# The C product of chunk 15 moved from DVE to GpSimd in a selective-scan ring on one Trainium2 core

## What is computed

```python
xp = jnp.einsum('bld,rd->blr', x, x_proj_w)
dt_in = xp[..., :DT_RANK]
B = xp[..., DT_RANK:DT_RANK + D_STATE]
C = xp[..., DT_RANK + D_STATE:]
dt = jax.nn.softplus(jnp.einsum('blr,dr->bld', dt_in, dt_proj_w) + dt_proj_b)
dA = jnp.exp(dt[..., None] * A)
dBx = dt[..., None] * B[:, :, None, :] * x[..., None]
# step: h = dA_t * h + dBx_t;  y = einsum('bdn,bn->bd', h, C_t)
y = jnp.moveaxis(ys, 0, 1) + D * x
```

## Time and profile before

| | us |
|---|---|
| median of 3 runs | 7002.88 |
| lowest, highest | 6997.77, 7003.49 |
| profiled execution, its own time | 6997.07 |
| its span, first to last instruction | 6995.4 |

### The profile page before, as it was taken

How to read it: one execution, slowest core, us unless ns; L and a number is a source line. 1 busy time by engine, 2 the same in 40 slices (tenths; PEclk the granted TensorE clock), 3 DMA queues, 4 the chain that set the end, 5 groups by cost and what they waited for, 6 DMA issues and landing times. The chain is left out here.

```text
span 6995.4 us, 109105 instructions
## 1 busy us (share of the span) xinstructions
PE 5921.1 (85%) x32339; PEld 5392.8 (77%) x32339; DVE 6184.9 (88%) x6216; ACT 4956.5 (71%) x13239; POOL 5960.5 (85%) x3596
## 2 busy tenths in 40 slices
PE   4658688888888888888888888888888888888887
PEld 3424588888888888888888888888888888888887
DVE  7863799999999999999999999999999999999996
ACT  4536677777777777777777777777777777777774
POOL 3420899999999999999999999999999999999995
PEclk8779899999999999999999999999999999999999
DMA  2430212222122211222212221122211222112220
GB/s 61 97 71 5 78 59 74 74 78 74 54 74 74 79 70 58 74 74 78 72 56 74 74 79 69 59 74 74 78 69 59 74 74 78 66 57 75 77 73 30
DMA packets 96273, 479.74 MB, mean 69 GB/s; under 512 B 13089, under 2 KB 17329, under 8 KB 87410
## 3 DMA queue, kind: packets, MB, share of 16 engines
q1 hardware_dynamic: 95602, 471.63, 19.5%
HBM read 328.35 MB, written 143.24 MB: 67 GB/s over the span
## 5 line engine op out<-in xcount | busy, mean ns | idle before, releaser
L1026 POOL TENSOR_TENSOR s_ring<-s_bc,s_u_t 128x820 f32<-128x820 f32 x2048 | 3623.6, 1788 | 3.5 <-DMA s_bc<-rows_bc 3.5
L944 ACT ACTIVATE s_decay<-s_dt_t,a_neg 128x205 f32<-128x205 f32 x8192 | 3045.8, 420 | 751.9 <-DVE s_ring L1088 570.1
L846 PE MATMUL s_y_ps<-s_ring,ident 128*128 128x205 f32 x16384 | 3284.6, 350 | 168.5 <-POOL s_ring L1032 79.3
L846 PEld LDWEIGHTS s_y_ps<-s_ring,ident 128*128 128x128 f32 x16384 | 2946.3, 198 | 302.4 <-POOL s_ring L1032 103.4
L1032 POOL TENSOR_TENSOR s_ring<-s_ring,s_bc 128x820 f32<-128x820 f32 x1024 | 1974.4, 1928 | 403.3 <-DVE s_ring L1082 397.3
L1082 DVE TENSOR_TENSOR_SCAN s_ring<-s_decay,s_ring 128x820 f32<-128x820 f32 x1024 | 1900.6, 1856 | 186.1 <-ACT s_decay L944 184.3
L1082 DVE TENSOR_TENSOR_SCAN s_decay<-s_decay,s_ring 128x820 f32<-128x820 f32 x1024 | 1908.5, 1864 | 120.1 <-ACT s_decay L944 98.4
L877 PE MATMUL s_xch<-s_x_t,w_low 128*128 128x205 f32 x8192 | 1512.0, 337 | 1.7 <-ACT s_x_t L975 0.6
L877 PEld LDWEIGHTS s_xch<-s_x_t,w_low 128*128 128x128 f32 x8192 | 1432.9, 190 | 5.8 <-DVE s_h L1144 1.1
L1088 DVE TENSOR_TENSOR s_ring<-s_decay,s_bc 128x820 f32<-128x820 f32 x1024 | 1035.6, 1011 | 35.2
L988 ACT ACTIVATE s_y_t<-s_xch,y_bias 128x205 f32<-128x205 f32 x512 | 217.0, 424 | 737.2 <-PE s_xch L877 737.2
(11 more groups left out here) (163 smaller groups left out, 4616.6 us busy)
## 6 DMA issues: line engine op xcount, KB each, us to landing
s_bc<-rows_bc SPq DMA_DIRECT2D x64, 3280.0 KB, 12.5
mixed<-t_res SPq DMA_DIRECT2D x32, 1024.0 KB, 10.0
s_x_in<-mixed SPq DMA_DIRECT2D x64, 512.0 KB
s_h<-mixed SPq DMA_DIRECT2D x64, 512.0 KB
before<-s_h SPq DMA_DIRECT2D x64, 512.0 KB
out<-s_h SPq DMA_DIRECT2D x64, 512.0 KB
s_x_in<-in_txt SPq DMA_DIRECT2D x64, 308.0 KB
s_h<-in_txt SPq DMA_DIRECT2D x64, 308.0 KB
```

The lines of the kernel that those rows point to most:

```text
L846: last = nc.tensor.matmul(y_ps, ident[:, :], ring[:, c % RING, n * LEN:(n + 1) * LEN], start=(c % 4 == 0 and n == 0), stop=(c % 4 == 3 and ...
L944: last = A.activation(decay[s % 2][:, n * LEN:(n + 1) * LEN], dt_t[:, par, j, :], ACT.Exp, scale=t["a_neg"][:, j, n0 + n:n0 + n + 1])
L1026: nc.gpsimd.tensor_tensor(ring[:, s % RING, :].rearrange("p (n l) -> p n l", n=CN), bc[:, par, n0:n0 + CN, :], u_t[:, par, j, :].unsqueeze ...
```

## The change

A tuple `ON_DVE` names the chunks whose product with C is on DVE: the odd ones without 15. POOL multiplies the other 17. The scan of chunk 15 writes into its ring slot, as for even chunks. Semaphores and counts follow: `pool_hc` counts 17 products an entry and `dve_hc` 15, and ACT waits before the decay of chunk 17 for the scan of chunk 15 instead of its product.

```diff
--- before.py
+++ after.py
@@ -637,6 +637,7 @@
 X_GROUPS = PREPARES + CONTINUES + ENDS
 X_STEP = len(X_ORDER) // 2
 RING = 8
+ON_DVE = tuple(s for s in range(1, CHUNKS, 2) if s != 15)
 EDGE = 512 - 2 * LEN
 LAG = 3
 
@@ -651,6 +652,18 @@
 
 LAST_ENTRIES = [(BATCH - 1, x_start(BATCH - 1), CONTINUES + ENDS), (BATCH, x_start(BATCH - 1) + 10, CONTINUES + ENDS),
                 (BATCH + 1, x_start(BATCH - 1) + 20, ENDS)]
+
+
+def by_dve(s):
+
+    return sum(c <= s for c in ON_DVE)
+
+
+def by_pool(s):
+    return s + 1 - by_dve(s)
+
+
+PER_DVE, PER_POOL = by_dve(CHUNKS - 1), by_pool(CHUNKS - 1)
 
 
 class Exchange:
@@ -703,7 +716,7 @@
 
 
         decay_done, dbx_done, scan_done, sum_done = sem("s_decay_done"), sem("s_dbx_done"), sem("s_scan_done"), sem("s_sum_done")
-        even_hc, odd_hc = sem("s_even_hc"), sem("s_odd_hc")
+        pool_hc, dve_hc = sem("s_pool_hc"), sem("s_dve_hc")
         y_done = sem("s_y_done")
         x_full = [sem(f"s_x_full{i}") for i in range(2)]
         x_empty = [sem(f"s_x_empty{i}") for i in range(2)]
@@ -839,7 +852,10 @@
 
             def sums(u, c):
 
-                wait(pe, odd_hc if c % 2 else even_hc, u * (CHUNKS // 2) + c // 2 + 1)
+                if c in ON_DVE:
+                    wait(pe, dve_hc, u * PER_DVE + by_dve(c))
+                else:
+                    wait(pe, pool_hc, u * PER_POOL + by_pool(c))
                 if c % 4 == 0:
                     wait(pe, y_done, u * ND + c // 4)
                 for n in range(CN):
@@ -848,8 +864,10 @@
                 last.then_inc(sum_done, 1)
 
             def chunk(u, par, s, x, scan, after):
-                if after if s < LAG else scan:
+                if s >= LAG and scan:
                     sums(u, s - LAG)
+                if s < LAG and after:
+                    sums(u - 1, s - LAG + CHUNKS)
 
             def add(v, par, r, x):
 
@@ -934,10 +952,13 @@
                 if not scan:
                     return
                 j, n0 = s // 4, CN * (s % 4)
-                if s % 2:
-                    wait(act, odd_hc, u * (CHUNKS // 2) + s // 2)
+                before = (s - 2) % CHUNKS
+                if before not in ON_DVE:
+                    wait(act, scan_done, u * CHUNKS + s - 1)
+                elif s < 2:
+                    wait(act, dve_hc, (u - 1) * PER_DVE + by_dve(before))
                 else:
-                    wait(act, scan_done, u * CHUNKS + s - 1)
+                    wait(act, dve_hc, u * PER_DVE + by_dve(before))
                 if s % 16 == 0:
                     wait(act, reset_done, u * 2 + s // 16 + 1)
                 for n in range(CN):
@@ -1030,12 +1051,12 @@
                 n0 = NS + CN * (c % 4)
                 wait(pool, scan_done, u * CHUNKS + c + 1)
                 nc.gpsimd.tensor_tensor(ring[:, c % RING, :], ring[:, c % RING, :],
-                                        bc[:, par, n0:n0 + CN, :].rearrange("p n l -> p (n l)"), ALU.mult).then_inc(even_hc, 1)
+                                        bc[:, par, n0:n0 + CN, :].rearrange("p n l -> p (n l)"), ALU.mult).then_inc(pool_hc, 1)
 
             def chunk(u, par, s, x, scan, after):
                 if scan:
                     inputs(u, par, s)
-                if (s - LAG) % 2 == 0:
+                if (s - LAG) % CHUNKS not in ON_DVE:
                     if s >= LAG and scan:
                         times_c(u, par, s - LAG)
                     if s < LAG and after:
@@ -1079,20 +1100,20 @@
                 g = u * CHUNKS + s
                 wait(dve, decay_done, g + 1)
                 wait(dve, dbx_done, g + 1)
-                V.tensor_tensor_scan(out=decay[1] if s % 2 else ring[:, s % RING, :], data0=decay[s % 2], data1=ring[:, s % RING, :],
+                V.tensor_tensor_scan(out=decay[s % 2] if s in ON_DVE else ring[:, s % RING, :], data0=decay[s % 2], data1=ring[:, s % RING, :],
                                      initial=0.0, op0=ALU.mult, op1=ALU.add).then_inc(scan_done, 1)
 
             def times_c(u, par, s):
                 n0 = NS + CN * (s % 4)
                 wait(dve, scan_done, u * CHUNKS + s + 1)
-                V.tensor_tensor(ring[:, s % RING, :], decay[1], bc[:, par, n0:n0 + CN, :].rearrange("p n l -> p (n l)"),
-                                ALU.mult).then_inc(odd_hc, 1)
+                V.tensor_tensor(ring[:, s % RING, :], decay[s % 2], bc[:, par, n0:n0 + CN, :].rearrange("p n l -> p (n l)"),
+                                ALU.mult).then_inc(dve_hc, 1)
 
             def chunk(u, par, s, x, scan, after):
 
                 if scan:
                     scan_chunk(u, par, s)
-                    if s % 2:
+                    if s in ON_DVE:
                         times_c(u, par, s)
                 if s == 2 and after:
                     block_output(u - 1, 1 - par, ND - 1)
```

## The result

| | before | changed |
|---|---|---|
| median, us | 7002.88 | 7034.23 |
| lowest, highest | 6997.77, 7004.98 (5 runs) | 7028.58, 7046.81 (5 runs) |
| span of the profiled execution | 6995.4 | 7026.9 |
| mean granted clock of TensorE | 0.946 | 0.939 |

The change makes the kernel slower by 31 us: ratio 1.0047, 95% interval 1.0032 to 1.0061. The forecast was 6934 us. The direction is wrong. The result lies inside the range of 6905 to 7045 us only because rival A (7042), which is nearest, set its upper end, and it got there in another way than rival A's, so that is luck.

A forecast was written before the change was run, and what follows sets the result against it. No engine is full: ACT's pace, POOL's backlog at product 2 of even entries and TensorE's half-clock stretches bound it. -24 x 3.15 + 6.3 = -69 us from 7002.88 gives 6934 us, range 6905 to 7045.

The forecast's parts named there:

- rival A: POOL's 1.1 us reaches PE at product 2 of every even entry, all half-clock stretches stay: 7042 us; chance 0.27.
- DVE's freed product is worth 0: At scan 17, which waits for ACT's decay: the 1.01 us an entry that DVE saves gains 0.
- POOL 1.1 us later through the backlog, product 2 of the even entry hit, no scan input late: POOL from product 16 to the next entry: +1.1 us a pair at product 2; input 2 keeps a 1.6 us margin.
- Sums of chunk 15, names and counts: PE takes these sums 3.7 us after POOL's product 15; added semaphore register instructions run behind a queue: both 0.
- The even entry's stretch gone, a pair 0.4 us shorter: PE's half-clock stretch after the 2.99 us wait disappears, -1.5 us; with POOL's +1.1 us, -0.4 us a pair.
- -2.75 us for 24 of the 28 pairs: Odd entries' half-clock stretches shrink as in the pair from entry 5; that pair's length becomes 191.4 us.
- the one short pair of the trace: Kernel before, pair from entry 5: 191.80 us, not 194.55, with parts of the odd entry's half-clock stretches at full clock.
- entry 5's position: Position against the clock's falls where a pair took 191.80 us; each earlier start was to move the kernel toward it.
- The bound "0 to -2.75": Gain per pair from the odd entry's half-clock stretches: 0 if they stay, up to -2.75 us.
- Start and end +6.3: Entries 0 to 3 and 63, outside the pair pattern, with POOL behind in all: 1.9 + 4 x 1.1 = +6.3 us.
- Rival B: Clock gives back what POOL takes, pairs stay 194.55 us: 7009 us; chance 0.18 together with a case of -5 us.
- the second stretch: Odd entry, PE at half clock after a 2.99 us wait for the normalised rows: 1.4 us lost a pair.

The follow-up runs named there:

- e6: Changed kernel with filler matmuls in TensorE's waits before `add`, `turn1`, `turn2` and `dt`; 6874.60 us, ratio to before 0.9800 to 0.9827.
- e2: Kernel before plus one extra, unused product on POOL behind the inputs of chunk 18, DVE's products kept; 7015.55 us, ratio to before 1.0004 to 1.0022.
- e3: Changed kernel with chunk 9 instead of chunk 15 multiplied on POOL; 7005.66 us, ratio to before 0.9994 to 1.0012.
- e1: Changed code with the old division, all 16 odd chunks on DVE; 7006.63 us, ratio to before 0.9993 to 1.0010.
- e9: Changed kernel with zero-adding matmuls only in TensorE's waits before `turn2` and `dt`; 7001.03 us, ratio to before 0.9992.
- e13: Kernel before with zero-adding matmuls only in TensorE's waits before `turn2` and `dt`; 7006.09 us, ratio to before 0.9999.
- e5: Kernel before with filler matmuls in TensorE's waits before `add`, `turn1`, `turn2` and `dt`; 6842.60 us, ratio to before 0.9753 to 0.9780.

## Why the prediction was wrong

- *DVE's freed product is worth 0*: right at the place that was worked out. Scan 17 waits for ACT.
- *POOL 1.1 us later through the backlog, product 2 of the even entry hit, no scan input late*: right, 1.04 us in e6 and in 20 of 27 even entries of the changed kernel. e2 shows it without DVE's part, e3 that the backlog is the condition.
- *Sums of chunk 15, names and counts*: 0, as said (3.8 us of margin; e1).
- *The even entry's stretch gone, a pair 0.4 us shorter*: it is gone in 20 of 27 even entries, and the 17 ordinary pairs are 0.23 us shorter. Behind a long odd entry it is back.
- *-2.75 us for 24 of the 28 pairs*: **this step failed.** Short pairs of the forecast length came (191.1 to 191.4, forecast 191.4), but only four of 27. I took the one short pair of the trace as a state that the kernel would move to and stay in. Neither holds. The kernel did not stay: no more than two short pairs follow each other (from 23 and 25), and the pair behind them is longer than any of the kernel before (195.3 to 202.0 us). And the way there, by which each earlier start was to move it toward entry 5's position, leads past positions where a pair is long: the pairs of entries 25 and 27 have their first stretch 6.345 and 6.343 us after scan 0, and take 191.14 and 201.98 us.
- *The missing term*: a new fall in a wait that had been harmless. Six pairs with stretches at `turn2` and after cost +30.6 us, where the sum had -66. The bound "0 to -2.75" was one-sided: I asked which stretches could go, and not which of PE's other waits could start one. e9 and e13 show that this term makes the measured loss: with it taken away the late product costs nothing that can be told from the kernel before.
- *Start and end +6.3*: 17.7 us measured up to entry 7. But e1, with the work of before, had 11.9 of it, so much of it is a difference between executions; with fillers it was 6.3 (e6 against e5). The sum also left out entries 4 to 6, which are in no term of it; by its own prices that is a few us.
- *Rival A* gave 7042 us and was the nearest, for another reason: its +1.1 us a pair is not in the pairs of the changed kernel (18 of 27 are shorter than 194.55), only in e6. That its 7042 lies near 7034 is luck. *Rival B*, the position against the falls holding the length of a pair, describes the kernel before and e3, and not the changed one.

Left open: why the second stretch goes away on one side of 6.34 us and not on the other, and what carries a pair to its position. The rows show where the kinds lie, not why; and only one execution of each kernel has such rows.
